# Attention on one Trainium2 core: the causal mask moves from a TensorE matmul to the VectorE row-maximum instruction

## The reference

```python
q = (x @ Wq.T).reshape(b, t, N_HEADS, HEAD_DIM).transpose(0, 2, 1, 3)
k = (x @ Wk.T).reshape(b, t, N_KV_HEADS, HEAD_DIM).transpose(0, 2, 1, 3)
...
q = _qknorm(q, q_scale)
k = _qknorm(k, k_scale)
...
scores = jnp.einsum('bhtd,bhsd->bhts', q, k) * scale
causal = jnp.tril(jnp.ones((t, t), dtype=bool))
scores = jnp.where(causal, scores, jnp.finfo(scores.dtype).min)
attn = jax.nn.softmax(scores, axis=-1)
out = jnp.einsum('bhts,bhsd->bhtd', attn, v)
```

## Time and profile before

| what | value |
|---|---|
| median of 3 runs | 999.92 us (998.39 to 1000.32) |
| span of the profiled execution | 997.6 us |
| TensorE matmul busy | 972.3 us, 97% |
| TensorE weight load busy | 854.1 us, 86% |
| VectorE busy | 533.0 us, 53% |
| ScalarE busy | 460.1 us, 46% |
| GpSimd busy | 306.8 us, 31% |

### The profile page before, as it was taken

The page is one execution under the profiler, slowest core; times in us unless marked ns, Lnnn a source line. Parts: engine busy times, 40 slices in busy tenths (PEclk is TensorE's granted clock), DMA queues, the critical chain, the costliest instruction groups (busy, mean ns, idle before and its releaser), DMA issues. The chain is left out here.

```text
span 997.6 us, 17492 instructions
## 1 busy us (share of the span) xinstructions
PE 972.3 (97%) x6116; PEld 854.1 (86%) x6122; DVE 533.0 (53%) x1132; ACT 460.1 (46%) x952; POOL 306.8 (31%) x268
## 2 busy tenths in 40 slices
PE   7999999999999999989999999999999999999998
PEld 5999999958888888856898899789788688888887
DVE  4734555455333333376866876886786633333333
ACT  1523444334333333335764664674673543333332
POOL 2110000023555555532121211212210245555553
PEclk7559999999999999999999999999999999999999
DMA  9735464011111111120010000000000111111111
GB/s 274 310 126 219 169 215 175 1 43 34 50 45 47 47 47 47 32 87 22 1 33 1 21 0 32 21 0 0 1 1 2 34 47 47 47 47 47 47 47 58
DMA packets 24052, 62.96 MB, mean 63 GB/s; under 512 B 2960, under 2 KB 13904, under 8 KB 21712
## 3 DMA queue, kind: packets, MB, share of 16 engines
q1 hardware_dynamic: 24016, 62.48, 18.6%
HBM read 61.43 MB, written 1.05 MB: 63 GB/s over the span
## 5 line engine op out<-in xcount | busy, mean ns | idle before, releaser
L699 DVE TENSOR_TENSOR f_h<-f_scaled,bank 128x512 f32<-128x512 f32 (+1 forms) x90 | 60.8, 676 | 183.6 <-POOL f_scaled L600 183.6
L789 PE MATMUL bank<-f_xt_hi,f_w_lo 128*128 128x512 f32 (+1 forms) x400 | 157.0, 393 | 0.0
L789 PE MATMUL bank<-f_xt_hi,f_w_hi 128*128 128x512 f32 (+1 forms) x400 | 156.6, 392 | 0.0
L600 POOL TENSOR_TENSOR f_scaled<-f_act,f_gate_rows 128x512 f32<-128x512 f32 (+1 forms) x90 | 113.5, 1262 | 135.5 <-ACT f_act L531 135.1
L538 ACT ACTIVATE f_h_hi<-f_h 128x512 fp32r<-128x512 f32 (+2 forms) x102 | 63.6, 624 | 183.9 <-DVE f_h L699 183.9
L377 PEld LDWEIGHTS bank<-cv_onehot,cv_raw 128*128 128x128 f32 x1024 | 141.4, 227 | 6.1 <-issue 5.6
L377 PE MATMUL bank<-cv_onehot,cv_raw 128*128 128x64 f32 x1024 | 141.2, 311 | 5.1 <-DMA cv_raw<-in_wconv 5.1
L300 DVE TENSOR_TENSOR cv_ws_lo<-bank,cv_ws_hi 128x512 fp32r<-128x512 f32 x64 | 81.7, 1276 | 80.7 <-ACT cv_ws_hi L223 80.6
L789 PE MATMUL bank<-f_xt_lo,f_w_hi 128*128 128x512 f32 (+1 forms) x400 | 123.7, 390 | 0.1
L968 ACT ACTIVATE at_prob<-bank,at_sbias,at_qrs 128x512 f32<-128x512 f32 (+3 forms) x128 | 77.6, 617 | 85.6 <-DVE at_sbias L1138 85.6
L806 PE MATMUL bank<-f_w_lo,f_h_hi 128*128 128x256 f32 (+1 forms) x400 | 113.2, 283 | 0.0
(11 more groups left out here) (177 smaller groups left out, 1994.6 us busy)
## 6 DMA issues: line engine op xcount, KB each, us to landing
cv_raw<-in_wconv SPq DMA_DIRECT2D x12, 2048.0 KB, 7.8
f_wraw<-in_w SPq DMA_DIRECT2D x44, 256.0 KB, 2.6
cv_raw<-in_wconv SPq DMA_DIRECT2D x6, 1024.0 KB, 20.3
f_wraw<-in_w SPq DMA_DIRECT2D x44, 128.0 KB, 2.4
at_wraw<-in_wqkv SPq DMA_DIRECT2D x3, 768.0 KB, 4.4
cv_x_dup<-in_x SPq DMA_DIRECT2D x4, 512.0 KB, 8.0
cv_raw<-in_wconv SPq DMA_DIRECT2D x4, 512.0 KB, 12.0
at_oraw<-in_wo SPq DMA_DIRECT2D x4, 512.0 KB, 3.6
```

Of the source, the lines that this page charges most:

```text
L600: g.tensor_tensor(scaled[half][:, cols], act[half][:, cols], gate_rows[:, half * HALF + cols.start:half * HALF + cols.stop], ALU.mult).the ...
L699: v.tensor_tensor(h_f[half][0:rows, cols], src[half][0:rows, cols], pu[half][0:rows, cols], ALU.mult)\
L789: mm = t.matmul(bank[half][0:rows, :], w, x, start=q == 0, stop=q == len(steps) - 1)
```

## The change

TensorE's mask matmul and the bf16 identity go. `causal` becomes a float32 tile of 128 x 512: zeros in the first 384 columns, the triangle in the last 128. VectorE's row maximum becomes `tensor_tensor_reduce`: it adds the mask's last 128(j+1) columns to the row of scores, writes the sum back to the same place in PSUM, and gives the maximum of the sum. Ahead of it stands an increment of a new semaphore `s_taken` that nobody waits for, which takes the wait for the scores.

```diff
-            g.memset(pm["ident_b"][:], 0.0).then_inc(s["const_done"], 1)
...
-            g.wait_ge(s["const_done"], 4)
-            for m in (pm["ident"], pm["ident_b"]):
-                g.affine_select(out=m[:], in_=m[:], compare_op=ALU.not_equal, fill=1.0, base=0,
-                                pattern=[[-1, P]], channel_multiplier=1)
-
-            g.affine_select(out=pm["causal"][:], in_=pm["causal"][:], compare_op=ALU.is_ge, fill=MASKED, base=0,
+            g.wait_ge(s["const_done"], 3)
+            g.affine_select(out=pm["ident"][:], in_=pm["ident"][:], compare_op=ALU.not_equal, fill=1.0, base=0,
+                            pattern=[[-1, P]], channel_multiplier=1)
+            diagonal = pm["causal"][:, (NQ - 1) * P:NQ * P]
+            g.affine_select(out=diagonal, in_=diagonal, compare_op=ALU.is_ge, fill=MASKED, base=0,
                             pattern=[[-1, P]], channel_multiplier=1)
...
                     v.wait_ge(s["s_ready"], g * NU * NQ + (NQ * u + (NQ if j < 2 else NQ - j)))
-                    v.tensor_reduce(smax[:, sl, j:j + 1], ps[bank][:, col:col + P * (j + 1)], AX_X, ALU.max)\
-                     .then_inc(s["max_done"], 1)
+                    v.sem_inc(s["s_taken"], 1)
+                    row = ps[bank][:, col:col + P * (j + 1)]
+                    v.tensor_tensor_reduce(row, row, pm["causal"][:, (NQ - 1 - j) * P:NQ * P], 1.0, -3.0e38,
+                                           ALU.add, ALU.max, smax[:, sl, j:j + 1]).then_inc(s["max_done"], 1)
...
                         triple(ps[bank][:, col:col + n], (qt_hi[:, sl, q], qt_lo[:, sl, q]),
-                               (kt_hi[:, b, 0:n], kt_lo[:, b, 0:n]), True, False)
-                        t.matmul(ps[bank][:, col + n - P:col + n], pm["ident_b"][:], pm["causal"][:],
-                                 start=False, stop=True).then_inc(s["s_ready"], 1)
+                               (kt_hi[:, b, 0:n], kt_lo[:, b, 0:n]), True, True).then_inc(s["s_ready"], 1)
...
-            "ident_b": sb("ident_b", [P, P], BF16),
-            "causal": sb("causal", [P, P], BF16),
+            "causal": sb("causal", [P, NQ * P], F32),
```

More of the change, by code:

```diff
@@ L872, in attention_phase @@
             "kt_hi_done", "kt_lo_done", "v_hi_done", "v_lo_done", "q_ready", "qsq_done", "qt_hi_done", "qt_lo_done",
-            "qsum_ready", "qsum_done", "qrs_done", "s_ready", "max_done", "bias_done", "exp_done", "rec_done",
+            "qsum_ready", "qsum_done", "qrs_done", "s_ready", "s_taken", "max_done", "bias_done", "exp_done", "rec_done",
             "prob_done", "pt_ready", "pt_hi_done", "pt_lo_done", "o_ready", "ot_hi_done", "ot_lo_done", "y_ready")}
```

## The result

The changed kernel takes 1001.15 us (median; 1000.17 to 1004.99) against 999.47 us (998.39 to 1000.32) for the kernel before beside it: a ratio of 1.0022, with an interval of 1.0015 to 1.0029. The forecast was 998.4, so it is a little slower where I had it a little faster. The profiled execution has a span of 1003.2 us against 997.6. It is the slowest of the twenty (1004.99 us), so its profile shows more of what follows than a median execution has.

A forecast was written before the change was run, and what follows sets the result against it. TensorE was taken to bound middle units by a narrow lead over a VectorE and ScalarE loop. Terms of -1.6, -1.35, +0.4, +0.2 and +0.8 gave -1.55 us, from 999.92 to 998.4 us; 8-in-10 range 995 to 1010.

The forecast's parts named there:

- the clock is no matter here: TensorE, whole kernel: granted clock full from the fourth slice on, so no term for it in the sum.
- The masks' worth on TensorE: Scores section of each unit: removing four mask matmuls saves 0.51 us, leaving TensorE alone needing 7.10 us.
- boundary: Between groups, where TensorE is full: one unit's masks go, about -0.45 us at each of three, -1.35 us.
- The loop, 7.30 us: VectorE and ScalarE's loop in a middle unit, were TensorE infinitely fast: 7.30 us before; 7.51 with the added reads.
- 0.08 for each read: VectorE's accumulator read after each of four maxima delays the next instruction by 0.08 us, 0.32 us a unit.
- middle steps: Four per group, 16 in all: 7.51 us against 7.61, so -0.40 us a group, -1.6 us in all.
- that which at_wkv_lo holds: Later GpSimd subtraction, which can hold another, now shifted bias: +0.2 us in each of four groups, +0.8 us.
- unit 2 to 3: Step lengthened by GpSimd's hold on unit 2's bias: +0.05 us, four times, +0.2 us.
- Rival 1: Accumulator read waits until its producer ends, 0.16 us per maximum, about +6 us: 1006 us; chance 0.24, including cases between.
- Rival 2: Increment costs up to 0.08 us behind a read at two of four maxima, loop 7.67: 1002.5 us; chance 0.15.
- Rival 3: Writing back into the PSUM bank it reads slows VectorE's maximum, +1.37 us a unit, +36 us: 1034 us; chance 0.07.
- Rival 4: VectorE's accumulator read is free, loop 7.30 us, -5.0 in 16 steps and -1.35 at boundaries: 993.5 us; chance 0.12.

The follow-up runs named there:

- filled kernel: Changed kernel plus six matmuls of zeros ahead of unit 0's values, inside TensorE's long wait in unit 2's step: 998.11 us, ratio 0.9989.
- no-mask kernel: Kernel before without its mask matmuls, with the old row maximum, scores not masked at all: 997.36 us (992.73 to 1001.16).
- no-mask kernel with the fill: Kernel before without its mask matmuls, scores unmasked, plus six matmuls of zeros ahead of unit 0's values: 992.18 us, ratio 0.9930.
- increment's kernel: Kernel before without mask matmuls, with six matmuls of zeros, plus the increment of s_taken ahead of each old row maximum: 993.12 us, ratio 0.9939.
- changed again: The changed kernel run once more with no edit, against the kernel before: 1000.77 us (999.68 to 1002.78), ratio 1.0017.

## Why the prediction was wrong

**The ledger.** Three terms, each from a pair of kernels: the masks off TensorE, 999.06 to 992.18, -6.9 us; VectorE's part on a TensorE so relieved, 992.18 to 998.11, +5.9, of which the increment is about 0.9; the clock, 998.11 to 1000.77, +2.7. Together +1.7. The kernels of the second pair ran on two chips; the kernels before beside them differ by 0.06 us. My sum had the first two terms, as -1.55 net, and they measure 998.11 - 999.12 = -1.0. It had nothing for the third, and that is what turns the sign.

**The step that failed** is in the first paragraph of the prediction: its granted clock is full from the fourth slice on, "so the clock is no matter here". A full clock in the trace of before shows that TensorE's idle time there is harmless, not that more of it would be. I had the place: the hold in unit 2, and I said that VectorE sets the pace there. What I didn't ask is what TensorE does meanwhile. At a full clock its longer wait costs nothing, and my sum priced it so. It is the longest wait of the phase, though, and it grew by 0.53 us, because its end is fixed by GpSimd and VectorE while TensorE reaches it earlier; behind it the clock fell in some groups. The filled kernel differs from the changed one only in that TensorE works in this wait, and there the clock holds and the time is 998.11 us. That it lies so near my 998.4 is in part luck of the starting point: I summed from 999.92, the median of three executions, and the kernel before beside it took 999.12. By differences it is -1.0 against -1.55.

**The masks' worth on TensorE, 0.51 us a unit**: the scores section now takes 573.73 - 571.77 = 1.96 us by the rows below, against 2.36. So 0.40 there, and 0.02 more in the query section behind it. The scores section is 1.96 us in the no-mask kernel too, and across a group's boundary, where TensorE is full, the no-mask kernel with the fill takes 27.17 us from scores to scores instead of 27.59. So the masks were worth 0.42, and the comparison with the values section made it 0.1 too much. The sum doesn't hang on it: 7.61 - 0.42 = 7.19 is still below 7.30. TensorE's timeline of the changed kernel:

```profile
571.77 0.49 PE L1231 MATMUL bank<-at_kt_hi,at_qt_hi 128*128 128x512 f32 x1
...
572.33 0.40 PE L1231 MATMUL bank<-at_kt_lo,at_qt_hi 128*128 128x512 f32 x1
...
573.73 0.45 PE L1231 MATMUL bank<-at_xt_hi,at_wq_hi 128*128 128x512 f32 x1
```

**The loop, 7.30 us, now 7.51**: 7.26 measured, and 7.51 measured, but the terms between are not mine. From the first maximum to its bias it is 574.31 - 572.92 = 1.39 us, against 579.63 - 578.37 = 1.26 with old maxima in the increment's kernel; the second pair takes 575.73 - 574.89 = 0.84, against 582.96 - 582.24 = 0.72. So 0.25 us for four maxima, 0.06 each on average, where I took 0.08 for each read. It isn't spread like that, however. The second maximum of a pair starts 573.54 - 572.92 = 0.62 us after the first, against 0.61 with the old ones: there the read costs 0.01. From the second maximum to the bias it is 574.31 - 573.54 = 0.77, against 0.66: the cost lies where the bias waits for the accumulated maximum, and the wider instruction's own extra time is in it. The increment, which I put at zero because at_pt_lo would hide it, costs 0.07. The errors nearly cancel; 7.51 is right partly by luck.

**What I said would be seen.** VectorE no longer waiting for the scores: wrong. The first maximum starts 0.69 us after at_pt_lo, not 0.60, and 572.92 is 0.19 us after the end of the last matmul of its row (572.33 + 0.40 = 572.73). By these starts the loop goes through TensorE: at_qt_lo (570.96 + 0.68 = 571.64), scores (571.77), increment, maximum. TensorE idle 0.4 us ahead of the scores: wrong as to place. The scores follow close, and the idle time is spread: by section lengths, values have 0.17 us more and the query sums 0.15. TensorE's busy time down by 29 us: wrong, it is 975.1 us (969.7 in the second profile) against 972.3. The modelled ends can cover small waits, and slow stretches add busy time; how much each makes wasn't separated.

**The places of the sum**, by the steps of the filled kernel and of the changed one's undisturbed groups: middle steps 7.51 (forecast 7.51), except that which at_wkv_lo holds, 7.70, so +0.19 (forecast +0.2, but I counted it in four groups, and at_wkv_lo runs in three); boundary 27.59 to 27.28, -0.31 (forecast -0.45); unit 1 to 2 7.10 for 6.97 to 7.04, +0.06 to +0.13 (forecast +0.10); unit 2 to 3 +0.06 to +0.08 in three groups (forecast +0.05), but 8.89 for 8.49 in the last, where the first maximum of unit 3 waits 0.34 us for its scores. Not in my sum at all was the step from unit 0 to 1 of the first group, 6.51 for 6.98. In the last group the middle steps fall to 7.42, more than I had. From the first maximum to the last the filled kernel is 1.9 us shorter than before (294.28 against 296.16), close to the -1.55. In the two profiles the rest of the difference lies ahead of the phase: its first maximum stands at 454.87 us instead of 453.95. It stands between 453.3 and 454.9 in the twelve profiles, and why isn't known.

**The rivals.** Rival 1 (the read waits for its producer's end) fell: the read and the next full-width instruction both start at 573.54, while the producer has until 572.92 + 0.70 = 573.62. I had built this rival on the section "The DRAIN you can't avoid" of the Trainium skill's page "VectorE: DVE Perf Modes", which also says that a next instruction that isn't held starts earlier, and sends the reader to "Two Vector instructions with no wait between them". By that section neither instruction is held here, and this row agrees. The 0.08 us came from the earlier trace rows, not from that page. Rival 2 is half right, and the measured time lies in its range (1000.5 to 1004), but not by its mechanism: the increment costs 0.07 us a unit, not at the second maximum of a pair as I had it (0.16) but on the way from the scores to the first. Rival 3 fell; this group of the changed kernel's attention phase answers to the earlier trace rows, 698 ns against 690:

```profile
L1134 DVE CUSTOM_DVE_ANT_0 bank<-bank,causal 128x512 f32<-128x512 f32 x32 | 22.3, 698 | 6.8 <-PE bank L1231 6.3 <-DVE X L1123 0.2
...
L1134 DVE DVE_READ_ACCUMULATOR2_ANT at_smax<- 128x1 f32 x128 | 18.1, 141 | 0.0
```

Rival 4 (the read is free) is right for the read between two maxima and wrong ahead of a bias: a middle unit takes 7.51 us, not 7.30. No rival had the clock.

**The hold itself.** A bias of two columns takes 1.25 to 1.40 us while GpSimd makes at_wo_lo, and 0.16 when it doesn't. The Trainium skill's page "SBUF — State Buffer", section "Who interferes with whom", says that a VectorE instruction with two SBUF inputs contends with a GpSimd one that reads SBUF; the bias reads at_smax and at_qrs, both there, and the trace agrees. Taking it away is worth 999.06 - 994.40 = 4.7 us to the kernel before and 1000.77 - 992.79 = 8.0 to the changed one, for which it also takes away the wait of 1.07 us behind which the clock fell. The same edit splits at_wkv_lo, which held another bias for 0.32 to 0.37 us in these two kernels, so the gain is that of both. The changed kernel with that edit, 992.79 us, is faster than either kernel without it.

**What stays open**: why the fall comes in one group or execution and not in another. TensorE's waits in unit 2 of the second group of the changed kernel:

```profile
552.28 0.44 PE L1231 MATMUL bank<-at_pt_hi,at_v_hi 128*128 128x384 f32 x1 [1.08 <-DVE at_pt_lo L1116]
...
553.70 0.39 PE L1231 MATMUL bank<-at_pt_hi,at_v_hi 128*128 128x256 f32 x1 [0.63 <-DVE at_pt_lo L1116]
```

They are as long as the third group's 1.07 and 0.63, yet the clock stayed full behind them and the step from unit 2 to 3 took 8.60 us. Falls behind unit 2's values stand in the profiles of the three runs with waits of 1.06 us or more there (changed, changed again, no mask) and in none of the nine others, so the longer wait seems to be needed, but it alone doesn't decide. The short fall of the first group is another matter: it stands in three profiles (changed, and the two of the changed kernel without the hold), begins in unit 2's scores, and TensorE's idle time of 0.60 to 0.63 us ahead of that unit's query sums (0.17 before) is as long in profiles without it (0.60 in changed again, 0.61 with the wait filled). Open too is what the changed kernel would be without the increment.

## What to carry to other kernels

When you relieve an engine that leads by little, it may no longer be the bound: sum the loop that takes its place, the smallest semaphore step included. Then look at the longest wait of the relieved TensorE rather than at its mean share, since its end can be fixed by others while TensorE reaches it earlier, and the clock can fall behind it; give that a rival of its own. A few matmuls of zeros in the wait show whether the clock is at stake, with the same fill in the kernel before as a control; where no wait is left they cost time. Here the better cure was to remove what the wait was for: a GpSimd instruction that held a bias of two columns.

## What the runs showed of the hardware

- TensorE's granted clock fell to its lower level behind waits of 1.06 to 1.15 us and, soon after them, 0.47 to 0.63 us, and stayed there for about 7 to 10 us, in some groups and executions and not in others. A fall of 3.4 us came in the first group without such a wait. In a median it cost 2.7 us; in the times it shows as spread: 8 us between executions of the no-mask kernel, under 1 with the wait filled.
- VectorE's accumulator read lasts 0.14 us and starts together with the next full-width instruction, which it delays by no more than 0.01 us. A bias that waits for the read's result comes 0.11 us later than behind the plain maximum.
- A masked maximum that writes back into its PSUM bank takes 698 ns for 512 columns and 330 for 128 (10.6 us for 32), against 690 and 279.
- A wait carried by a semaphore increment ahead of the instruction adds 0.11 to 0.12 us on the way from TensorE's matmul to VectorE's maximum, of which 0.07 show in a middle unit.
- A GpSimd subtraction of 256 columns takes 0.74 us, one of 1024 columns 2.39.
